# Gather groups of four blocks with one short group of two per tile: 332 blocks instead of 352

## The reference, cut to what matters

```python
dst = minimum((1250 * uniform(key, (40000,)) ** 2.0).astype(int32), 9999)   # then sorted
msgs = x[src]
out = x @ root + bias
for r in range(8):
    mask = (edge_type == r)
    sums = segment_sum(msgs * mask[:, None], dst)
    cnt = segment_sum(mask, dst)
    out = out + (sums / maximum(cnt, 1.0)[:, None]) @ weight[r]
u = out
z = concatenate([u, x]) @ w_gate + b_gate
h = tanh(u) * z + x * (1.0 - z)
```

## Time and profile before

| | us |
|---|---|
| median of three timed runs | 2202.74 (2202.08 to 2203.47) |
| profiled execution, its own time | 2193.12 |
| its span, first to last instruction | 2191.1 |
| TensorE matmul busy | 2031.3 (93%) |
| VectorE busy | 1294.1 (59%) |
| ScalarE busy | 997.8 (46%) |
| GpSimd busy | 938.7 (43%) |

### The profile page before, as it was taken

One profiled execution on the slowest core, in us unless ns is written; L12 is line 12 of the kernel. 1 busy time (PEld: TensorE's weight loads), 2 busy tenths in 40 slices (PEclk: granted clock), 3 DMA queues, 4 the chain that ended last, 5 costly groups with the idle time before them and its releaser, 6 DMA issues. The chain is left out here.

```text
span 2191.1 us, 28288 instructions
## 1 busy us (share of the span) xinstructions
PE 2031.3 (93%) x9505; PEld 1608.8 (73%) x9505; DVE 1294.1 (59%) x2246; ACT 997.8 (46%) x1546; POOL 938.7 (43%) x821
## 2 busy tenths in 40 slices
PE   7999999999999999999899899999799669999970
PEld 6777778778888888877677677677488558888860
DVE  8578488832222222139999999999888742222215
ACT  3211122222222222249999999999743313333322
POOL 0000044565655555337777788788400022221212
PEclk9999999999999999999999999999999879999995
DMA  5223487777777778679988898897265479998449
GB/s 186 99 81 134 140 270 254 260 250 255 253 252 252 257 259 256 228 236 316 328 272 315 308 332 312 311 314 270 79 182 183 165 296 322 331 309 289 97 75 187
DMA packets 159792, 521.03 MB, mean 238 GB/s; under 512 B 33628, under 2 KB 34012, under 8 KB 157616
## 3 DMA queue, kind: packets, MB, share of 16 engines
q1 hardware_dynamic: 85616, 310.54, 40.5%
q0 software_dynamic: 74048, 208.88, 31.8%
HBM read 394.35 MB, written 154.71 MB: 251 GB/s over the span
## 5 line engine op out<-in xcount | busy, mean ns | idle before, releaser
L208 PE MATMUL psum<-w_hi,xnT_hi 128*128 128x512 f32 (+1 forms) x1592 | 419.1, 398 | 5.0 <-PEq L225 2.5
L208 PE MATMUL psum<-w_lo,xnT_hi 128*128 128x512 f32 (+1 forms) x1592 | 421.5, 395 | 0.0
L208 PE MATMUL psum<-w_hi,xnT_lo 128*128 128x512 f32 (+1 forms) x1592 | 413.6, 394 | 0.0
L846 POOL DMA_INDIRECT sorted_rows<-acc x313 | 344.6, 1101 | 116.7 <-issue 84.7
L573 ACT ACTIVATE work<-psum 128x512 f32<-128x512 f32 (+1 forms) x150 | 89.8, 598 | 663.4 <-PE psum L208 663.4
L208 PEld LDWEIGHTS psum<-w_lo,xnT_hi 128*128 128x128 f32 (+1 forms) x1592 | 296.6, 186 | 73.4
L208 PEld LDWEIGHTS psum<-w_hi,xnT_lo 128*128 128x128 f32 (+1 forms) x1592 | 294.7, 186 | 72.3
L208 PEld LDWEIGHTS psum<-w_hi,xnT_hi 128*128 128x128 f32 (+1 forms) x1592 | 291.6, 186 | 74.3 <-issue 4.1
L930 POOL DMA_INDIRECT w_hi<-y_rows,sort_row x176 | 237.9, 1352 | 67.0 <-issue 42.7
L930 POOL DMA_INDIRECT w_lo<-y_rows,sort_row x176 | 232.0, 1318 | 65.6 <-issue 46.3
L1012 DVE SCALAR_TENSOR_TENSOR w_hi<-w_hi,sort_recip,y_hi 128x1024 fp32r<-128x1024 f32 x176 | 223.6, 1282 | 26.2 <-ACT y_hi L976 21.4
(11 more groups left out here) (312 smaller groups left out, 2623.8 us busy)
## 6 DMA issues: line engine op xcount, KB each, us to landing
split_experts<-acc SPq DMA_DIRECT2D x128, 512.0 KB, 4.2
ring<-split_experts SPq DMA_DIRECT2D x16, 4096.0 KB, 16.6
w_raw<-in_wchunks SPq DMA_DIRECT2D x86, 512.0 KB, 4.9
y_rows<-work SPq DMA_DIRECT2D x144, 256.0 KB, 3.0
acc<-in_wchunks SPq DMA_DIRECT2D x64, 512.0 KB, 5.9
work<-local_rows SPq DMA_DIRECT2D x26, 384.0 KB, 4.1
sum_rows<-work SPq DMA_DIRECT2D x22, 256.0 KB, 3.0
acc<-in_bias SPq DMA_DIRECT2D x10, 512.0 KB, 5.3
```

Of the source, the lines that this page charges most:

```text
L208: i = pe.matmul(to[:rm, :], x_[:, k, m * P:m * P + rm], w_[:, s, k * HALF:(k + 1) * HALF], start=(n == 0), stop=(n == 3 * KD - 1))
L846: pool.indirect_dma_start(sorted_dram, IndirectOffsetOnAxis(ap=e_dest[:, c:c + 1], axis=0), e_rec[:, c, :], None, bounds_check=BLOCKS * P ...
```

## The change

A tile's edges are counted in half groups of two blocks. A tile takes long groups of four blocks, and where its half groups are odd, one short group of two blocks for its last edges. The list holds 78 long groups and behind them 10 short ones: 332 blocks. Short groups are given to tiles from the last one downwards, and where there are more long groups than 78, two short groups in a row serve as one.

The gather stage keeps 44 passes of two groups. Passes 8, 19, 30, 41 (those with weight pieces) and 43 take short groups, four blocks a pass, all others long ones. In a pass with pieces one piece now stands ahead of each block, the first included. ORDER, FIRST and COLUMN translate a group and a block in program order to their places in the list. In `starts` and `positions` instructions are added that compute the short groups' starts and tiles and shift a tile's last edges to its short group. The diff, without allocations, renamings and unchanged parts:

```diff
-GROUPS = (EDGES + TILES * (GROUP * P - 1)) // (GROUP * P)
-BLOCKS = GROUPS * GROUP
+SHORT = GROUP // 2
+SHORT_GROUPS = TILES
+LONG_GROUPS = -(-((EDGES + TILES * (SHORT * P - 1)) // (SHORT * P) - SHORT_GROUPS) // 4) * 2
+GROUPS = LONG_GROUPS + SHORT_GROUPS
+BLOCKS = LONG_GROUPS * GROUP + SHORT_GROUPS * SHORT
...
-PASSES = BLOCKS // SLOTS
+PASSES = GROUPS // 2
...
-                    link(v.tensor_scalar(t_count, t_count, float(GROUP * P - 1), None, ALU.add))
+                    link(v.tensor_scalar(t_count, t_count, float(SHORT * P - 1), None, ALU.add))
                     link(v.tensor_copy(t_int, t_count))
-                    link(v.tensor_scalar(t_int, t_int, (GROUP * P).bit_length() - 1, None, ALU.logical_shift_right))
-                    link(v.tensor_copy(t_groups, t_int))
+                    link(v.tensor_scalar(t_int, t_int, (SHORT * P).bit_length() - 1, None, ALU.logical_shift_right))
+                    link(v.tensor_scalar(t_odd_i, t_int, 1, None, ALU.bitwise_and))
+                    link(v.tensor_scalar(t_int, t_int, 1, None, ALU.logical_shift_right))
+                    v.tensor_copy(t_groups, t_int)
+                    v.tensor_copy(t_odd, t_odd_i)
+                    v.memset(t_odd_start, 0.0)
                     link(v.memset(t_start, 0.0))
                     for t in range(1, TILES):
+                        v.tensor_tensor(t_odd_start[:, t:t + 1], t_odd_start[:, t - 1:t], t_odd[:, t - 1:t], ALU.add)
                         link(v.tensor_tensor(t_start[:, t:t + 1], t_start[:, t - 1:t], t_groups[:, t - 1:t], ALU.add))
...
+                    v.tensor_tensor(long_used, t_start[:, TILES - 1:TILES], t_groups[:, TILES - 1:TILES], ALU.add)
+                    link(v.tensor_tensor(t_shift, t_start, t_groups, ALU.add))
+                    link(v.scalar_tensor_tensor(out=t_shift, in0=t_shift, scalar=2.0, in1=t_odd_start,
+                                                op0=ALU.mult, op1=ALU.add))
+                    link(v.tensor_scalar(t_shift, t_shift, float(-SHORT * P), float((BLOCKS - SHORT) * P), ALU.mult, ALU.add))
+                    link(v.scalar_tensor_tensor(out=t_tail, in0=t_groups, scalar=float(GROUP * P), in1=t_off,
+                                                op0=ALU.mult, op1=ALU.subtract))
                     link(v.scalar_tensor_tensor(out=t_off, in0=t_start, scalar=float(GROUP * P), in1=t_off,
                                                 op0=ALU.mult, op1=ALU.add))
+                    link(v.tensor_scalar(short_f, group_f[:, LONG_GROUPS:GROUPS], -1.0, float(GROUPS - 1), ALU.mult, ALU.add))
+                    link(v.tensor_scalar(short_i, group_i[:, LONG_GROUPS:GROUPS], 1, None, ALU.logical_shift_right))
+                    link(v.tensor_copy(group_f[:, LONG_GROUPS:GROUPS], short_i))
+                    link(v.tensor_scalar(group_f[:, LONG_GROUPS:GROUPS], group_f[:, LONG_GROUPS:GROUPS],
+                                         float(LONG_GROUPS // 2), None, ALU.add))
                     for t in range(1, TILES):
+                        v.scalar_tensor_tensor(out=short_tile, in0=short_f, scalar=t_odd_start[:, t:t + 1], in1=short_tile,
+                                               op0=ALU.is_ge, op1=ALU.add)
                         link(v.scalar_tensor_tensor(out=l_tile, in0=group_f, scalar=t_start[:, t:t + 1], in1=l_tile,
                                                     op0=ALU.is_ge, op1=ALU.add))
+                    at = l_tile[:, LONG_GROUPS:GROUPS]
+                    v.tensor_scalar(short_f, group_f[:, LONG_GROUPS:GROUPS], long_used[:, 0:1], None, ALU.is_lt)
+                    link(v.tensor_tensor(at, at, short_tile, ALU.subtract))
+                    link(v.tensor_tensor(at, at, short_f, ALU.mult))
+                    link(v.tensor_tensor(at, at, short_tile, ALU.add))
...
                 def positions(first, last):
                     for t in range(first, last):
                         link(v.tensor_scalar(e_mask, e_tile, float(t), None, ALU.is_equal))
                         link(v.tensor_tensor_scan(e_scan, e_ones, e_mask, 0.0, ALU.mult, ALU.add))
+                        link(v.tensor_scalar(e_tail, e_scan, t_tail[:, t:t + 1], t_shift[:, t:t + 1], ALU.is_gt, ALU.mult))
+                        link(v.tensor_tensor(e_scan, e_scan, e_tail, ALU.add))
                         link(v.scalar_tensor_tensor(out=e_scan, in0=e_scan, scalar=t_off[:, t:t + 1], in1=e_mask,
                                                     op0=ALU.add, op1=ALU.mult))
                         link(v.tensor_tensor(e_pos, e_pos, e_scan, ALU.add))
...
         PIECES_AT = {TILES - 2: RELATION_CHUNKS + 1, 2 * TILES - 1: RELATION_CHUNKS + 2, 3 * TILES: RELATION_CHUNKS + 3,
                      4 * TILES + 1: CH_GATEU}
 
+        SHORT_PASSES = (*PIECES_AT, PASSES - 1)
+        ORDER, FIRST, COLUMN = [], [0], []
+        for i in range(PASSES):
+            for h in range(2):
+                short = i in SHORT_PASSES
+                n = sum((g >= LONG_GROUPS) == short for g in ORDER)
+                at, size = (LONG_GROUPS * GROUP + n * SHORT, SHORT) if short else (n * GROUP, GROUP)
+                ORDER.append(LONG_GROUPS + n if short else n)
+                COLUMN += range(at, at + size)
+                FIRST.append(len(COLUMN))
+        assert sorted(COLUMN) == list(range(BLOCKS))
+
+        def size_of(g):
+
+            return FIRST[g + 1] - FIRST[g]
...
-                                            IndirectOffsetOnAxis(ap=sort_row[:, j:j + 1], axis=0),
+                                            IndirectOffsetOnAxis(ap=sort_row[:, COLUMN[j]:COLUMN[j] + 1], axis=0),
...
-                def lane_distance(j):
-
-                    if j % GROUP == 0 and j >= GROUP:
-                        act.wait_ge(hot_done, j // GROUP)
-                    act.activation(apart[:, j % GROUP, :], lanes[:, :], ACT.Square, bias=sort_local[:, j:j + 1], scale=-1.0)\
+                def lane_distance(g, k):
+
+                    if k == 0 and g >= 1:
+                        act.wait_ge(hot_done, g)
+                    at = COLUMN[FIRST[g] + k]
+                    act.activation(apart[:, k, :], lanes[:, :], ACT.Square, bias=sort_local[:, at:at + 1], scale=-1.0)\
                 def one_hot(g):
 
-                    act.wait_ge(apart_done, GROUP * (g + 1))
+                    n = size_of(g)
+                    act.wait_ge(apart_done, FIRST[g + 1])
                     if g >= 2:
-                        act.wait_ge(pe_done, GROUP * (g - 1))
-                    act.activation(hot[:, g % 2, :, :], apart[:, :, :], ACT.Relu, bias=1.0, scale=-1.0).then_inc(hot_done, 1)
+                        act.wait_ge(pe_done, FIRST[g - 1])
+                    act.activation(hot[:, g % 2, 0:n, :], apart[:, 0:n, :], ACT.Relu, bias=1.0, scale=-1.0).then_inc(hot_done, 1)
...
-                    for b in range(SLOTS):
-                        j = i * SLOTS + b
-                        if b == 1:
+                    for n, (g, j) in enumerate((g, j) for g in (2 * i, 2 * i + 1) for j in range(FIRST[g], FIRST[g + 1])):
+                        b, k = j % SLOTS, j - FIRST[g]
+                        if n == 1:
...
-                        if b % 2 == 1 and pieces:
-                            c, q = pieces[b // 2]
+                        if pieces:
+                            c, q = pieces[n]
                             act.wait_ge(mm_done, c * TILES)
                             hi_piece(act, c, 0, q)
+                        act.wait_ge(landed[b], PLACED[b] + 16 * (j // SLOTS) + 16)
...
-                        if j + GROUP < BLOCKS:
-                            lane_distance(j + GROUP)
-                            if j % GROUP == GROUP - 1:
-                                one_hot(j // GROUP + 1)
+                                       scale=sort_recip[:, COLUMN[j]:COLUMN[j] + 1]).then_inc(hi_done, 1)
+                        if g + 1 < GROUPS:
+                            if k < size_of(g + 1):
+                                lane_distance(g + 1, k)
+                            if k == size_of(g) - 1:
+                                for late in range(size_of(g), size_of(g + 1)):
+                                    lane_distance(g + 1, late)
+                                one_hot(g + 1)
...
-                    v.wait_ge(pe_done, GROUP * g + GROUP)
-                    tile = v.value_load(group_tile[0:1, g:g + 1], min_val=0, max_val=TILES - 1)
+                    v.wait_ge(pe_done, FIRST[g + 1])
+                    tile = v.value_load(group_tile[0:1, ORDER[g]:ORDER[g] + 1], min_val=0, max_val=TILES - 1)
...
-                        for j in range(GROUP * g, GROUP * (g + 1)):
+                        for j in range(FIRST[g], FIRST[g + 1]):
                             b = j % SLOTS
-                            if b % 2 == 1 and pieces:
-                                lo_piece(v, pieces[b // 2][0], 0, pieces[b // 2][1])
+                            if pieces:
```

(40 more changed lines are left out.)

9 lines of the change are left out of this document (4 added, 5 removed).

## The result

The changed kernel takes 2187.25 us (median of 6 runs, 2184.26 to 2191.63), the kernel before 2202.41 (6 runs, 2198.01 to 2206.98): ratio 0.9949, 95% interval 0.9930 to 0.9968. (The recorded ratio is not the quotient of the two medians, which is 0.9931.) It is faster, by 7 to 15 us. The forecast was 2189.7, in a range from 2182 to 2198.5.

What follows compares the result with a forecast made beforehand. Long passes balanced between engines, VectorE busiest in piece passes; 15.3 us saved there and in pass 43, less 2.4 for the clock, gives 13: 2180 us profiled, plus 9.6 for the timed median, 2189.7; range 2182 to 2198.5.

Steps and rivals of the forecast that it cites:

- L: Landing time of piece 2's load in passes 8, 19, 30, 41: 4.9, 4.9, 5.5, 6.3 us; at 7.6 everywhere, 6.5 us gained.
- the clock: TensorE at half clock lasting into passes 9, 20, 31: 1 us each, 2.4 us net lost, bounds 0 and 4.5.
- The long passes: Gather stage's 39 passes of eight blocks: same instructions, denser transfers, costed at zero; 13.4 and 13.2 us.
- Pass 43: Last gather pass, no pieces: four blocks less of VectorE work, 12.53 us becomes 7.7.
- the prediction's cut: Gather passes are timed from the first VectorE multiply-subtract of each pass.
- VectorE's floor: VectorE's own work in short piece passes: 12.4 us in 8 and 19, 11.8 in 30 and 41.
- the hand-offs: VectorE standing for ScalarE's copy of piece 0 at the pass head: 0.7, 0.3, 1.3, 1.3 us in passes 8, 19, 30, 41.
- Bookkeeping: Added sort instructions in the products stage, 4.8 us in starts and 9 in positions: hidden, cost zero, bound 3 us.
- the loads are the bound: Rival, 15%: in short passes L stays at 6.3 to 7.6 us though the stream pauses; gain 2 to 8 us, 2197.
- The reason given: Blocks gathered just before passes 8 and 19 are empty, so the stream pauses and piece 2 was taken to land in 4.9 us.

Runs made afterwards that it cites:

- the second execution: The changed kernel run again unaltered, compared with the kernel before: 2185.97 us, ratio 0.9945, gather stage 597.0 us.

## Why the prediction was right, and where it was not

**The direction, the place and the time were right**, the time with luck. The gain I worked out was 12.9 us; the medians show 15.2, the ratio 11.2, and the stage 7.2 and 9.9 us in two executions. Of a profiled execution I expected 2180 us; the two took 2187.53 and 2182.33. I had added 9.6 us to come from a profiled execution to a median, and with the changed kernel that difference was -0.3 and 3.6. The piece passes came out too long and the 9.6 too large, and the two errors largely cancel in the 2189.7.

**By its own signs** the forecast failed in part. Passes 8 and 19 were to take 14 to 15 us and 41 up to 17; they took 16.21, 18.03 and 17.53 (15.59, 16.65 and 16.93 in the second execution). It was to be wrong if a load landed in over 7 us, and that of pass 19 took 8.0. The upper end of the range is also mis-added: with L = 7.6 the passes gain 6.5 us, and with the clock at its bound of 4.5 there are 2 us left, not 4, so 2200.7 and not 2198.5. And VectorE is busy 96% of passes 1 to 7 by the earlier trace rows, not 94%.

**Confirmed as sized.** The long passes are unchanged though denser: nine take 118.53 us, against 119.00 in the earlier trace rows. Pass 43 went, by the prediction's cut, from 12.53 to 7.20 (7.7 was forecast). VectorE's floor and the hand-offs came out (0.56, 0.55, 1.36, 1.35 against 0.7, 0.3, 1.3, 1.3). Bookkeeping is hidden: `starts` lasts from 113.64 to 125.17 us, 4.8 more than before as forecast, the batches it pushes are ready in time for the counts at 129.74, and the stage starts at 967.3. The second instruction of `positions` added per tile, and the first:

```profile
L777 DVE TENSOR_TENSOR acc<-acc 128x313 f32<-128x313 f32 x10 | 4.9, 487 | 0.3
L776 DVE TENSOR_SCALAR acc<-acc 128x313 f32<-128x313 f32 x10 | 4.4, 442 | 0.4
```

9.3 us, against 9 forecast, none of it on TensorE's path.

**The term that was mis-sized is L**, the landing of piece 2. I took 4.9, 4.9, 5.5 and 6.3 us, it was 6.5, 8.0, 5.8 and 6.9, so the four passes and pass 43 took 75.4 us and not 69.5: 9.4 gained and not 15.3. In the second execution the misses are 1 to 1.6 us in passes 8 and 19 and next to nothing in 30 and 41. The reason given was wrong in time, not in kind. The stream does pause for the empty blocks of passes 8 and 19, but eight blocks ahead, where they are gathered (1070 to 1075 us for pass 8); when piece 2 is loaded, from 1079.0, it is filling again. My rival "the loads are the bound", 15%, describes the piece passes better than the forecast did. The runs without the loads and with half of them show the price (12.7 to 15.3 us and 4.2 to 6.7 in the four passes), and that with an early piece shows that an earlier start alone doesn't help.

**The clock** cost 3.5 us by the run that kept TensorE busy, against 3 taken (2.4 net of what was there). By rows alone passes 9 and 10 take 28.09 against 27.47 and pass 20 14.47 against 12.63, 2.5 us more than in the kernel before. Pass 42 is 0.5 longer too (13.25 against 12.76), but at a granted clock of 0.87 in both, so that is not the clock's.
The Trainium skill's rule (TensorE: Matmul & The Clock Gate, "HAM oscillation — how this bites in real kernels") says that such bursts fall back each time; the trace now agrees for all four short passes, 19 included (0.57). In the run that kept the engine busy the clock was 1.00 in all four; what the falls cost is a few us and not whole passes.

**What stays open** is why the medians show 1 to 8 us more than the stage does. The part behind the stage varies by as much: it takes 616.1, 619.0 and 627.6 us in the three profiled executions of before, 618.7 and 616.5 in the changed kernel's two. The eight other profiles, whose code is the same there, have 615.5 to 625.8. The ten with 332 blocks average 619.4, the three of before 620.9, so little suggests that the change makes that part quieter; so few executions do not rule it out.

## What to carry to other kernels

Work that is dropped beside a load was also that load's cover: price the pass by the landing time that is left uncovered, and drop work where nothing is being waited for, in passes that another engine or the same engine bounds. Sixteen blocks less gave 4 and 6.6 us in the passes that load weights, and 18.5 us in four passes that don't, of which the piece passes, with full gathers beside them, gave 3.8 back. A gap in a prefetched stream shows up as many blocks early as the prefetch is deep, so here it gave no room to a load issued when the gap was consumed.
